# Edge-attribute sums of a graph network: the second half added by an accumulating DMA instead of by GpSimd

## What is computed

```
edge_index = jnp.stack([src, dst])
x = _layernorm(x + _L0_gnn_ref(x, edge_index, ...), axis=-1)
x = _layernorm(x + _L1_gnn_ref(x, src, dst, edge_attr_16, ...), axis=-1)

def _mp_layer(x, src_f, dst_f, ea_f, W, b):
    n = x.shape[0]
    m = jnp.concatenate([x[dst_f], x[src_f], ea_f], axis=1) @ W.T + b
    agg = jax.ops.segment_sum(m, dst_f, num_segments=n)
    return jax.nn.relu(agg)
```

## Time and profile before

| | us |
|---|---|
| median of 3 runs | 1153.56 |
| lowest and highest of them | 1153.36, 1153.74 |
| span of the profiled execution | 1151.4 |
| TensorE busy | 973.9 (85%) |
| VectorE busy | 718.9 (62%) |
| ScalarE busy | 391.3 (34%) |
| GpSimd busy | 131.4 (11%) |

### The profile page before, as it was taken

One profiled execution on the slowest core, in us unless ns is written; L12 is line 12 of the kernel. 1 busy time (PEld: TensorE's weight loads), 2 busy tenths in 40 slices (PEclk: granted clock), 3 DMA queues, 4 the chain that ended last, 5 costly groups with the idle time before them and its releaser, 6 DMA issues. The chain is left out here.

```text
span 1151.4 us, 19166 instructions
## 1 busy us (share of the span) xinstructions
PE 973.9 (85%) x7566; PEld 582.8 (51%) x7566; DVE 718.9 (62%) x1328; ACT 391.3 (34%) x750; POOL 131.4 (11%) x150
## 2 busy tenths in 40 slices
PE   0247877978688778999999999998999998999993
PEld 0246776868677665545555444443433443444441
DVE  5797989999999943623434755553465554334434
ACT  2485688887877720200000010213320104110000
POOL 4022223343222320000000000000000000000001
PEclk9868988989888977999999999998999998999997
DMA  6325546656545439953775435755036755037740
GB/s 165 57 74 206 177 130 242 199 177 195 174 125 181 177 127 292 377 235 140 317 278 211 183 120 234 276 219 224 15 126 249 286 192 224 19 147 280 286 173 23
DMA packets 63701, 216.77 MB, mean 188 GB/s; under 512 B 28320, under 2 KB 41627, under 8 KB 50067
## 3 DMA queue, kind: packets, MB, share of 16 engines
q1 hardware_dynamic: 55588, 164.52, 39.7%
q0 software_dynamic: 8016, 50.95, 12.3%
HBM read 170.69 MB, written 44.74 MB: 187 GB/s over the span
## 5 line engine op out<-in xcount | busy, mean ns | idle before, releaser
L1382 PE MATMUL PM<-Aring,Xop 128*128 128x512 fp8e4 (+1 forms) x1960 | 398.5, 363 | 0.0
L1382 PEld LDWEIGHTS PM<-Aring,Xop 128*128 128x128 f16 x1960 | 181.4, 98 | 216.7 <-issue 16.3
L821 PE MATMUL PW<-Aring 128*128 128x52 fp8e4 (+3 forms) x2151 | 120.9, 220 | 66.5 <-ACT F L889 64.0
L1907 ACT ACTIVATE F<-PH,bag 64x512 f32<-64x512 f32 (+1 forms) x39 | 25.5, 658 | 370.3 <-PE PH L1601 370.2
L821 PEld LDWEIGHTS PW<-Aring 128*128 128x128 fp8e4 x2151 | 114.8, 105 | 70.7 <-ACT F L889 66.5
L1382 PE MATMUL PM<-Ares,Xop 128*128 128x512 fp8e4 x588 | 138.1, 390 | 2.7 <-ACT Xop L1946 1.3
L1740 DVE TENSOR_SCALAR S<-PM 128x256 f32<-128x256 f32 (+1 forms) x75 | 31.4, 418 | 112.7 <-PE PM L1382 95.8
L1382 PEld LDWEIGHTS PM<-Ares,Xop 128*128 128x128 f16 x588 | 56.2, 100 | 71.7 <-issue 9.8
L1531 POOL DMA_DIRECT2D out<-dd x12 | 9.0, 754 | 705.8 <-DVE dd L1702 705.8
L889 ACT ACTIVATE F<-PW 128x392 uint16<-128x392 f32 x196 | 84.6, 513 | 11.0 <-PE PW L821 9.6
L679 DVE TENSOR_TENSOR Aring<-Ares 128x4096 uint16<-128x4096 uint16 x31 | 70.8, 2285 | 6.4 <-PE PW L821 6.1
(11 more groups left out here) (158 smaller groups left out, 1233.0 us busy)
## 6 DMA issues: line engine op xcount, KB each, us to landing
Aring<-adj SPq DMA_DIRECT2D x72, 1568.0 KB, 9.6
adj<-Aring POOLq DMA_DIRECT2D x12, 1568.0 KB, 5.9
adj<-Xop POOLq DMA_DIRECT2D x12, 1568.0 KB, 6.3
Ares<-adj SPq DMA_DIRECT2D x6, 1568.0 KB, 21.4
rc<-ea_sum SPq DMA_DIRECT2D x36, 128.0 KB, 5.7
Aring<-adj SPq DMA_DIRECT2D x4, 784.0 KB, 4.4
rc<-rc_d SPq DMA_DIRECT2D x12, 256.0 KB, 9.5
eaf<-in_erow SPq DMA_DIRECT2D x60, 51.0 KB, 2.0
```

What stands on the lines that cost most here:

```text
L821: last = nc.tensor.matmul(PW[begun % RING][:, c:c + 52 * (z - y)].rearrange("p (d v b) -> p d v b", d=z - y, b=2), lo[:, h % 2, i, :].bitc ...
L1382: last = nc.tensor.matmul(o, x[:, h, :], rhs, start=h == 0, stop=h == NT - 1)
L1907: nc.scalar.activation(F[0:64, c:c + w], PH[b % 2][0:64, 0:w], ACT.Relu, bias=t["bag"][:, 4 + conv:5 + conv]).then_inc(s_hr, 1)
```

## The change

The add on GpSimd (L585) and its semaphore go. The even half is stored as it is, once ScalarE has copied it (`first_half`). The odd half is stored by a second DMA of GpSimd that adds its elements to those in DRAM (`second_half`); it waits until the first has landed, and it is the one that increments `s_eo`. It is not issued right behind the first, but at the start of GpSimd's next turn, or before a third one would be open.

```diff
-        s_add = sem("s_add")
+        s_half = [sem(f"s_half{i}") for i in range(2)]
...
+            def first_half(st):
+
+                n = stage_width(st)
+                g.wait_ge(s_eas, st + 1)
+                g.dma_start(m["ea_sum"][:, st * SW:st * SW + n], eas[:, st % 2, 0:n]).then_inc(s_half[st % 2], 16)
+
+            def second_half(st):
+
+                n = stage_width(st)
+                g.wait_ge(s_half[st % 2], 16 * (st // 2 + 1))
+                g.dma_start(m["ea_sum"][:, st * SW:st * SW + n], odd[:, st % 2, 0:n],
+                            accum_op=ALU.add).then_inc(s_eo[st % 2], 16)
+
+            halved = []
...
             for h in range(NH + 2):
+                while halved:
+                    second_half(halved.pop(0))
                 if h % 2 and h // 2 + 5 < TS:
...
                     for st in sums_after(h - 1):
-                        n = SW if st < NST - 1 else LASTW
-                        g.wait_ge(s_eas, st + 1)
-                        nc.gpsimd.tensor_tensor(eas[:, st % 2, 0:n], eas[:, st % 2, 0:n], odd[:, st % 2, 0:n],
-                                                ALU.add).then_inc(s_add, 1)
-                        g.wait_ge(s_add, st + 1)
-                        g.dma_start(m["ea_sum"][:, st * SW:st * SW + n], eas[:, st % 2, 0:n]).then_inc(s_eo[st % 2], 16)
+                        if len(halved) == 2:
+                            second_half(halved.pop(0))
+                        first_half(st)
+                        halved.append(st)
+            while halved:
+                second_half(halved.pop(0))
```

## The result

The changed kernel takes 1148.93 us (median; 1145.65 to 1150.16) against 1153.56 for the kernel before. The medians alone differ by 4.6 us. The ratio on record for the runs is 0.9952, with a 95% interval of 0.9939 to 0.9965: 5.5 us faster (4.0 to 7.0), where the prediction had 14. The direction held, the size did not: two fifths of the expected gain arrived. The time lies in the wide range (1133 to 1151), outside the one of the forecast itself (1133 to 1145), and beside the 1148.5 of rival 1.

The account below looks back on a forecast made before the run. VectorE was taken to bound the build, TensorE 510 to 1130 us. Build -12 + 1 = -11 and handover -3 make -14: 1153.56 - 14 = 1139.6 us; forecast 1133 to 1145 (0.62), range 1133 to 1151.

Parts of the forecast that it names:

- rival 1: Handover: adding DMA lands late among SyncE's loads, TensorE idles, clock falls; +6 instead of -3, 1148.5 us; chance 0.14.
- The add's price: Build: GpSimd's adds lengthen VectorE's two-input products; removing them saves 12 us (bounds 10.1 to 18.8).
- The rule on shared SBUF access: VectorE's two-SBUF-input instructions contend with GpSimd instructions reading SBUF; the added DMA issues cost such products nothing.
- The adding DMA: GpSimd's accumulating store in each of 25 stages: landing 3.3 us (2.1 to 4.2), issue 0.55 us (up to 1.1).
- ScalarE: Build, stage 21: copies wait for stage 19's rows to be stored, 3 us late; charged 1.0 us (0 to 2.5).
- The stage stores: Build: stage stores queued on GpSimd behind the second halves lose nothing, covered by VectorE's release.
- The handover: From build to first layer, 420 to 510 us: later barrier, but TensorE's gap closes; -3.0 us (-4 to +6).
- the cap: Second layer's start: factors' slack of 4.0 us, loads 1.3 us later, lets at most 2.7 to 4 us pass.
- Rival 2: Build: DMA issues stop VectorE as adds do, giving the 12 us back, 1151.6 us; chance 0.12 (all or half).
- Rival 3: ScalarE's wait for stage s-2: slow accumulating DMA, from about 7.5 us of landing; +9, 1162.5 us; chance 0.12.

Follow-up runs that it names:

- e5: Kernel before without GpSimd's 25 adds: odd half left out, only the even half stored, fallback flag held at zero; 1134.62 us.
- e8: Changed kernel with early factor loads and four buffers for the halves of the sums instead of two; ratio 0.9872.
- e4: Kernel before with the last stage (24) alone stored in halves, the second adding; the other 24 stages still added by GpSimd; 1161.17 us, 1.0058.
- e10: Changed kernel run once more, unchanged, for a second profile and times; median 1147.89 us, ratio 0.9955.
- e1: Changed kernel with the first two factor loads of the second layer issued ahead of the adjacency loads; 1138.96 us, 0.9878.
- e2: Kernel before, adds kept, with the first two factor loads of the second layer issued ahead of the adjacency loads; ratio 0.9996.

## Why the prediction was right or wrong

**The add's price: right in kind, too small.** The products' means came back to 1219 and 1225 ns as said. I had 12 us, from 0.53 us per add; VectorE's work became 16.4 us shorter in the changed kernel and 16.2 in e5, where the whole build gained 18.2, next to the bound of 18.8 that I had worked out for an add that stops VectorE for all its length. The two shapes of the earlier trace rows give 10 of these 16; the rest fell on instructions that I had not counted: from 143 us on, the operands of L686 took 3.0 us less, the unpacking (L703, L704) 1.3 and L644 1.2.

**The rule on shared SBUF access held.** The trace agrees with what the prediction took from the Trainium skill ("SBUF — State Buffer", Who interferes with whom): 50 DMA issues where there were 25, and VectorE's two-input products at their undisturbed length.

**The adding DMA: within its bounds.** I took 3.3 us for its landing (2.1 to 4.2) and 0.55 for its issue (0.55 to 1.1): 2.7 and 0.87 measured. What I undersized was the plain first half: 2.1 taken, 3.5 in the median and up to 7.9 measured. At eight of them, issued within 1.8 us behind a stage store, GpSimd waited 5.4 to 7.7 us each; at none of the others did it wait more than 4.8.

**ScalarE: place right, price about right.** I had ScalarE wait 3 us at stage 21; it waited 2.88 us there, until 382.88. The longest of its five waits, 4.61 us until 395.08, was at stage 23. I charged 1.0; e8 shows at most 1.25. The build came 16.2 us earlier in the profile where I had 11.

**The stage stores: put at nothing, and not nothing.** I looked at the place behind the add at 390.50, where the stage store had to wait for VectorE anyway, and wrote "the cover is VectorE's release". At the last pair of stage stores there is hardly any: the first stands at 423.07 with 0.19 us of idle time ahead of it and no VectorE in it, and only the second waited for VectorE, 1.07 us. There the halves of stages 22 and 23 held the stores back by 1.8 to 3.1 us against the unpacking, where in e5, without halves and without adds, stores and unpacking moved by the same 18.2 us. The landing of the last half, the sums and the loads behind them start from these stores.

**The handover: each step right but the last.** Predicted and measured in e4, where it stands alone: barrier 433.5 and 432.2; end of the sums' wait 437 and 436.75; TensorE's gap closed, both; TensorE 3.4 us earlier at the end of its rounds, and 4.8 measured, 3.9 without the head start of its build. Then the step that failed, the cap that the second layer's factors put on the gain. I wrote of the factors: "a slack of 4.0 us", the loads "start when the large load has landed, 1.3 us later; so at most 2.7 to 4 us of gain passes", and took 3.0. The row behind it was the right one. The large load is the first link only by way of the reciprocals' store queued behind it, and by my own landing times (450.5 to 452 for 449.6) its delay was 0.9 to 2.4 us, which leaves less than the 2.7 to 4 that I wrote. But above all:
- the factors came 3.6 us later, not 1.3. Of this, 1.3 are the loads' start (452.44 against 451.12), and 2.3 that the transfers from there to the factors took longer, which nothing in my sum allowed for;
- with TensorE 4.8 us earlier and the factors 3.6 later, the slack of 4.0 became idle time: 4.8 + 3.6 - 4.0 = 4.4, and 4.23 measured. I had treated the cap as something that clips a gain. I did not put the two shifts against each other, which would have shown an idle TensorE at that place, and with it the fall of the clock that I had priced at 6.2 us for the first layer's gap. It cost 1.2 us in e4's profile (11.93 against 10.74), 2.2 in e10's.
By the ratios, this one stage costs +6.7 us where I had -3.0; with the early factors it gives -1.8.

So the missing 8.5 us are the cap: with it taken away (e1) the change measured -14.1, and the same edit is worth nothing without the change (e2). In the changed kernel the cap works on the build's gain too, which I had not asked about: TensorE was 16.9 us earlier and its factors 8.2.

That e1 has the very size of the forecast is luck. In its profile the build ends 15.2 us earlier where I had 11, and TensorE reaches the second layer 15.3 us earlier, so the handover gave 0.1 where I had 3.4. The two errors nearly cancel.

**Rivals.** Rival 1 had the right events, an idle TensorE and its clock down after the handover, and nearly the right time (1148.5), at the wrong place: I looked for them ahead of the third round, where the gap did close. Rival 2 (issues stop VectorE) is refuted by the means. Rival 3 needed 7.5 us of landing; it was 2.7.

**Open.** The profiled run of e4 is 2.5 us above that of before, its median 6.7 above. The second profile of the changed kernel lost 2.1 us more than the first at the gap and 1.6 ahead of it; for e4 there is no second profile. So more than half of e4's 6.7 us stands in no trace. Why the adjacency transfers take 2 to 3 us longer in the kernels with the last stage in halves, and which wait holds the build 2 to 3 us above that without adds, is not settled.

**A version that is faster than both** is the changed kernel with the first two factor loads ahead of the adjacency loads: 1138.96 us, 1.2% below the kernel before and 0.7% below the change as it was made.

## What to carry to other kernels

A small add on GpSimd can cost VectorE most of its length when VectorE is the bound (0.65 us of busy time for an add of 0.75 here); giving it to an adding DMA is worth that, if nothing that is needed next has to wait for the first half's landing. Where work moves earlier on an engine, put every input that it meets next beside it with its own new time: if engine and input move apart, the slack does not merely cap the gain, it becomes idle time and then a lower clock. A small load that is needed first must not be issued behind 16 MB that are needed later.

## What the runs showed of the hardware

- An adding DMA of 33 KB (GpSimd's queue, rows in DRAM) lands in 2.3 to 3.6 us, median 2.7; the plain stores of the kernel before took 2.3 in the median (1.7 to 8.5), the plain first halves 3.5 (1.8 to 7.9). Its issue takes 0.87 us of GpSimd, a plain one 0.54.
- Twenty-five adds of GpSimd lengthened VectorE's 616 instructions of the build by 16.2 us, 25 more by another 11.8, and the second ones left the two products of VectorE as long as one add per stage had made them (1538 and 1554 ns for one of them) and lengthened others. Twenty-five more DMA issues in their place lengthened nothing (359.30 and 359.45 us).
- An idle time of 4.23 to 5.24 us ahead of one product of TensorE made it 11.89 to 12.90 us long instead of 10.74; in the changed kernel the granted clock was 0.76 and 0.90 in the 10 us around it.
- A load of 1312 KB issued 5.6 us earlier (419.98 instead of 425.62) took 17.2 us instead of 12.8 and landed only 1.2 us earlier (437.2 and 438.4), with the DMA engines busy for 0.83 or more of every 2 us until 434 and 436 us.
